# Decoder layer with cross-attention: where ScalarE makes the second part of a key or query piece

## The reference

```
q = split_heads(x @ Wq.T); k = split_heads(ctx @ Wk.T); v = split_heads(ctx @ Wv.T)
scores = einsum('bhqd,bhkd->bhqk', q, k) / sqrt(16)
out = einsum('bhqk,bhkd->bhqd', softmax(scores), v)      # 8 x 16 heads x 512 x 1601
x = layernorm(x + out @ Wo.T)
```

## Time and profile before

| | |
|---|---|
| median of 3 runs | 1775.92 us (1768.82 to 1776.91) |
| profiled execution, own time | 1775.18 us |
| its span, first to last instruction | 1773.4 us |
| PE busy | 1635.7 us, 92% |
| DVE busy | 1235.8 us, 70% |
| ACT busy | 1059.2 us, 60% |
| POOL busy | 163.5 us, 9% |

### The profile page before, as it was taken

How to read it: one execution, slowest core, us unless ns; L and a number is a source line. 1 busy time by engine, 2 the same in 40 slices (tenths; PEclk the granted TensorE clock), 3 DMA queues, 4 the chain that set the end, 5 groups by cost and what they waited for, 6 DMA issues and landing times.

```text
span 1773.4 us, 25671 instructions
## 1 busy us (share of the span) xinstructions
PE 1635.7 (92%) x9786; PEld 611.3 (34%) x9786; DVE 1235.8 (70%) x1811; ACT 1059.2 (60%) x1987; POOL 163.5 (9%) x150
## 2 busy tenths in 40 slices
PE   5664988999999999999999999999999999999875
PEld 4341322333233333343343323333334324332232
DVE  4555766787778867787778777786778777777322
ACT  1110666676666766666666666666666666666740
POOL 5410100010001000110001000110001000000000
PEclk9775999999999999999999999999999999999987
DMA  4343416060705234161707061342507050600000
GB/s 127 84 102 87 83 49 113 6 122 24 131 25 93 64 78 78 38 106 27 128 16 132 26 119 38 68 90 64 92 1 135 22 82 25 107 2 1 4 24 16
DMA packets 99936, 116.59 MB, mean 66 GB/s; under 512 B 20811, under 2 KB 85196, under 8 KB 99813
## 3 DMA queue, kind: packets, MB, share of 16 engines
q1 hardware_dynamic: 97076, 113.89, 32.1%
q10 hardware_dynamic: 2736, 1.06, 0.2%
HBM read 80.12 MB, written 34.78 MB: 65 GB/s over the span
## 4 chain that ended last, share of the span: by engine, by line
PE 78%; issue 4%; ACT 4%; DVE 3%; DMA 1%; ACTq 0%; POOLq 0%; POOL 0%; SPq 0%; DVEq 0%
PE banks L1052 21%; PE values L1069 21%; PE banks L1029 11%; PE work L937 4%; PE work L951 4%; ACT xprobs L1165 4%; PE work L907 4%; PE work L958 3%; PE work L964 3%; PE work L892 3%; PE work L967 1%; PE work L943 1%; DVE xneg_max_pieces L1353 1%; PE work L976 1%; DMA ctxT_b<-in_ctxT 1%
## 5 line engine op out<-in xcount | busy, mean ns | idle before, releaser
L1165 ACT ACTIVATE xprobs<-banks 128x512 f32<-128x512 f32 x1664 | 902.6, 594 | 464.0 <-PE banks L1052 449.3
L1353 DVE TENSOR_REDUCE xneg_max_pieces<-banks 128x2 f32<-128x1024 f32 x768 | 909.2, 1220 | 273.2 <-PE banks L1029 271.0
L1052 PE MATMUL banks<-xq_stacks,xk_stacks 99*128 99x512 bf16 (+1 forms) x1664 | 523.1, 385 | 34.5 <-ACT xprobs L1165 23.0
L1069 PE MATMUL values<-xprobs,xv_rows 128*17 128x512 f32 x3328 | 437.9, 598 | 1.0 <-ACT xprobs L1165 1.0
L1052 PEld LDWEIGHTS banks<-xq_stacks,xk_stacks 99*128 99x128 bf16 (+1 forms) x1664 | 127.9, 97 | 427.4 <-ACT xprobs L1165 281.4
L1029 PE MATMUL banks<-xk_stacks,xq_stacks 49*128 49x512 bf16 (+1 forms) x2048 | 252.5, 339 | 14.5 <-DVE xneg_max_pieces L1353 9.9
L1029 PEld LDWEIGHTS banks<-xk_stacks,xq_stacks 49*128 49x128 bf16 x2048 | 56.7, 94 | 285.7 <-DVE xneg_max_pieces L1353 164.5
L1418 POOL TENSOR_TENSOR xk_parts<-xk_rest,xk_parts 128x401 bf16<-128x401 f32 (+1 forms) x64 | 58.9, 921 | 700.9 <-ACT xk_parts L1130 700.9
L1069 PEld LDWEIGHTS values<-xprobs,xv_rows 128*17 128x17 f32 x3328 | 55.1, 95 | 119.9 <-issue 118.5
L1413 POOL TENSOR_TENSOR xrstd<-xrstd,mhalf 128x4 f32<-128x4 f32 x23 | 23.2, 1010 | 665.2 <-DVE xrstd L1225 665.2
L1116 ACT ACTIVATE xk_parts<-work 128x401 bf16<-128x401 f32 (+1 forms) x64 | 32.4, 507 | 57.0 <-PE work L937 57.0
(11 more groups left out here) (250 smaller groups left out, 1092.5 us busy)
## 6 DMA issues: line engine op xcount, KB each, us to landing
xk_stacks<-key_parts_dram SPq DMA_DIRECT2D x192, 200.1 KB, 11.9
key_parts_dram<-xk_parts SPq DMA_DIRECT2D x144, 100.0 KB, 1.7
xq_stacks<-parts_dram SPq DMA_DIRECT2D x192, 64.0 KB, 8.0
ctxT_a<-in_ctxT SPq DMA_DIRECT2D x4, 1601.0 KB, 7.4
ctxT_b<-in_ctxT SPq DMA_DIRECT2D x4, 1601.0 KB, 8.6
parts_dram<-xq_parts SPq DMA_DIRECT2D x48, 128.0 KB, 1.9
key_parts_dram<-xk_parts SPq DMA_DIRECT2D x48, 100.2 KB, 7.9
xa<-in_x SPq DMA_DIRECT2D x8, 512.0 KB, 14.3
```

The costliest lines, as they stand in the source:

```text
L1052: pe.matmul(scores[n % SRING], kst[0:ROWS[par], k, h2, par, t * P:(t + 1) * P], qst[0:ROWS[par], k, h2, par, :], start=True, stop=True).th ...
L1069: last = pe.matmul(av[32 * j:32 * j + HD + 1, :], vals[:, k, t, gr * GH + j, :], probs[:, sl % 2, j, :], start=t == 0, stop=t == XKT - 1)
L1165: nc.scalar.activation(probs[:, sl % 2, j, :], scores[n % SRING], ACT.Exp).then_inc(exped, 1)
L1353: nc.vector.tensor_reduce(nmp[:, of % 2, j2, :, q, piece], pairs[n % MRING][:, :, :], AX.X, ALU.max, negate=True).then_inc(mxr, 1)
```

## The change

`act_later` for the piece that ended in the slot before moves from behind exp 1 to behind exp 3, ahead of the high part of a piece that ends in this slot.

```diff
             act_exp(m, t, 1)
             if t == 0 and m:
                 act_values_out(m - 1)
-            if sl and ends_at(sl - 1):
-                act_later(MAIN, ends_at(sl - 1))
             if in_between(sl):
                 act_job(MAIN, in_between(sl))
             act_exp(m, t, 2)
             act_exp(m, t, 3)
+            if sl and ends_at(sl - 1):
+                act_later(MAIN, ends_at(sl - 1))
             if ends_at(sl):
                 act_job(MAIN, ends_at(sl))
```

## The result

| | before | after |
|---|---|---|
| median | 1774.95 us (9 runs, 1768.82 to 1776.91) | 1785.47 us (9 runs, 1780.69 to 1796.71) |
| span of the profiled execution | 1773.4 us | 1791.1 us |

The ratio is 1.0075, 95% interval 1.005 to 1.010. The change makes the kernel slower, where 0.2% faster (1772.3 us) was forecast. The runs also spread twice as wide as before, 16 us against 8; the profiled one is among the long ones.

The account below looks back on a forecast made before the run. PE was taken to set the time, busy 192.59 of 194.12 us a batch, with room on ACT. Terms of -2.9 and -0.7 us gave -3.6 us, so a median of 1772.3 us, range 1764 to 1780.

Parts of the forecast that it names:

- The gain: In slots 51 and 12, PE would wait less for ACT once the copy is moved: -3.6 us in all.
- Slot 51: Without the copy ahead, exp 2, exp 3 and the following V start 0.41 us earlier: 7 x 0.41 = 2.9 us gained.
- Slot 12: Without the copy ahead of x2T, PE's query matmuls take 1.02 us instead of 1.12: 7 x 0.10 = 0.7 us gained.
- The new place: Behind exp 3, the copy fits ACT's idle time before the high part, or delays exp 0 harmlessly: price nothing.
- the read-write bubble: Memory latency between ACT instructions behind exp 3; with no overlap the high part is 0.08 us late, losing 2.2 us.
- POOL and SP: Middle parts and stores come 1.1 to 2.5 us later, but waits and slack cover the stack loads: price nothing.
- The first: Chance 0.12: S0 in slot 0 waits for late-landing row maxima, leaving -0.7 us or nothing: 1775.9 us.

## Why the prediction was wrong

*The gain was right in place and size.* Slot 51: 0.42 us shorter for 0.41 forecast. Slot 12: 0.11 for 0.10, though slot 13 gives 0.05 of it back. With slot 23 left out the whole is 0.998, where 3.6 us of 1775 is 0.998.

*The new place costs nothing on ACT and PE, as forecast.* Slots 1, 11, 35 and 36 with a high part behind the copy have the length they had; so have slots 2, 14, 23 and 37. The high part behind a copy still starts when PE's piece is done, after 0.05 us of idle time (0.48 before), and slot 12's query matmuls take 1.02 us. The weighing of the read-write bubble comes out on the side of the rows: no lateness of the high part shows in any slot.

*The step that failed* is in the part on POOL and SP: "After slot 22's piece SP waits 6.3 us for PE's scores before it loads the first half of the stacks, more than the 1.5 us by which the stores come later." The wait does cover the stack loads: it shrinks from 6.3 to 4.4 us, and they start at slot 22 + 14.35 in both kernels. But between the stores and that wait, SP's list holds the context load, which waits for nothing of its own that is late and so takes over the whole delay. The prediction does not name this load: it has slack for its own reader, a batch later, and I did not ask what it would now meet. The delay was under-sized too: it is 1.97 us, the distance from the old to the new start of the copy. The term "Price: nothing" for POOL and SP measured about +20.8 us in the profiled execution, and 0.95% (1.0075 against 0.998), some 17 us, between the change and the run without slot 23's move.

*The rivals.* The first named the right victim, the row maxima, at the wrong place (slot 0), where nothing is lost. For the price of a late landing I had one row, the 1.6 us of an 8 KB DMA that ran with little beside it, and took it as fixed. No rival let a transfer that comes later delay another one that had not moved.

*What in the trace of before pointed to it:* the single wait of 1.6 us for the maxima in batch 0, and the context load itself, with 7.4 us to landing on the page of before, inside which the maxima are issued:

```profile
ctxT_a<-in_ctxT SPq DMA_DIRECT2D x4, 1601.0 KB, 7.4
```

The Trainium skill has the rule, "DMA: Bandwidth & Descriptors", section "Issuing engines are not separate DMA queues": transfers issued by ACT and SP run on the same 16 engines and interleave. The packets' times fit engines that the two share: the first of the 12 on ACT's queue ran 1.4 us after issue with the context load out of the way, 3.2 to 3.8 us after it with the load 2.7 us ahead, as before, and 4.0 to 5.6 us after it with the load 0.8 us ahead, as in the change. They do not interleave at once, though: in the 3.2 us from issue on, 201 packets of SP's queue ran before the first of ACT's.

**Still open.** Beyond the share of the stack loads it is open why the wait is 1.3 us in one batch and 4 in another of the same kernel, and why batch 0 keeps its long wait with the stack loads held. Where the packets of the maxima are held up, between their issue and their first packet, was not measured; the runs show the dependence on the start and the packets' times, not the cause inside the DMA hardware.

## What to carry to other kernels

When an instruction moves, follow its semaphore to the in-order DMA queue that waits for it, and list every transfer behind that wait, not only those that carry its data. For each ask two things: is it still in time, and which small transfer that PE waits for will now share the DMA engines with it? In this kernel the large prefetch had slack and was harmless once it was issued at the release of its buffer, ahead of stores that wait for another engine.

## What the runs showed of the hardware

- The packets of an 8 KB load in two DMAs of ACT's queue were done 2.2 us after its first issue when alone (10.1 to 12.3 after slot 22), 3.5 to 4.2 us with 1.6 MB issued 2.7 us ahead on SP's queue, and 7.6 us at worst (10.1 to 17.7, batch 3 of the change) with that load 0.8 us ahead and stack loads behind. That a small load could come 5 us late in this way I had not expected.
- A wait of PE of 4 us was followed by 6.8 us at a granted clock of 0.50, so the wait cost nearly twice its length (7.05 us in slots 25 and 26 of batch 3). In all runs together, waits of 1.8 to 3.4 us for the maxima were followed by 3.4 or 6.8 us at 0.50, and waits of up to 1.7 us left the clock at 1.00.
